# Relative position tiles: key units of the next tile alternate with query units of this one, and the square between them lies transposed in every other tile

## The reference

```python
dist_idx = pos_l - pos_r + M - 1
pos_emb = dist_emb[dist_idx]                            # [512, 512, 16]
rel_q = jnp.einsum('bhld,lrd->bhlr', q, pos_emb)
rel_k = jnp.einsum('bhrd,lrd->bhlr', k, pos_emb)
scores = (scores + rel_q + rel_k) / jnp.sqrt(D)
```

## Time and profile before

| | |
|---|---|
| median of 3 runs | 2111.92 us (2110.01 to 2112.20) |
| the profiled execution | 2123.17 us |
| its span in the trace | 2121.5 us |
| TensorE matmuls busy | 1641.8 us, 77% of the span |
| VectorE busy | 1129.5 us, 53% |
| ScalarE busy | 1032.1 us, 49% |
| DMA, mean over the span | 247 GB/s |
| TensorE's mean granted clock | 0.89 of full |

### The profile page before, as it was taken

The page is one execution under the profiler, slowest core; times in us unless marked ns, Lnnn a source line. Parts: engine busy times, 40 slices in busy tenths (PEclk is TensorE's granted clock), DMA queues, the critical chain, the costliest instruction groups (busy, mean ns, idle before and its releaser), DMA issues. The chain is left out here.

```text
span 2121.5 us, 32639 instructions
## 1 busy us (share of the span) xinstructions
PE 1641.8 (77%) x11256; PEld 1204.0 (57%) x11256; DVE 1129.5 (53%) x3008; ACT 1032.1 (49%) x2029; POOL 537.5 (25%) x628
## 2 busy tenths in 40 slices
PE   6758420089898899978899899858989989889881
PEld 3325320078787788767778788734555555555550
DVE  6666434213344444313444344447888887888860
ACT  3424304044343343443334344358887887887860
POOL 2343342200100000001010000053043644634534
PEclk9878655589999999979999999969999999999995
DMA  6574465688789678788887777589889989999831
GB/s 202 176 239 145 144 192 139 194 208 276 274 276 300 241 259 300 231 262 300 307 301 259 244 256 258 220 286 325 259 253 322 295 270 311 294 281 325 292 111 40
DMA packets 227380, 523.34 MB, mean 247 GB/s; under 512 B 37328, under 2 KB 83920, under 8 KB 221712
## 3 DMA queue, kind: packets, MB, share of 16 engines
q1 hardware_dynamic: 201856, 414.22, 60.3%
q0 software_dynamic: 24208, 98.65, 14.3%
q10 hardware_dynamic: 1152, 8.39, 1.0%
HBM read 371.27 MB, written 203.42 MB: 271 GB/s over the span
## 5 line engine op out<-in xcount | busy, mean ns | idle before, releaser
L986 DVE TENSOR_TENSOR rel_out<-rl,rel_tile 128x1024 f32<-128x1024 f32 x256 | 305.9, 1221 | 225.9 <-PE rl L1038 177.9
L1254 ACT ACTIVATE scores<-scores,row_least 128x512 f32<-128x512 f32 x512 | 365.6, 717 | 27.9 <-DVE row_least L1288 27.7
L1288 DVE CUSTOM_DVE_ANT_1 scores<-sc,rq 128x512 f32<-128x512 f32 x512 | 336.3, 687 | 33.6 <-issue 27.9
L1390 PE MATMUL pt<-ident,scores 128*128 128x128 f32 x2048 | 322.7, 281 | 34.0 <-ACT probsT L1259 17.5
L963 ACT COPY rel_tile<-rl 128x1024 f32<-128x1024 f32 x256 | 249.7, 1017 | 180.6 <-PE rl L1038 169.8
L1059 PE MATMUL up<-rowsT,w_b 128*128 128x256 f32 x1280 | 322.1, 396 | 3.3 <-DMA w_b<-in_w 3.3
L1072 PE MATMUL dn<-w_b,hid 128*128 128x256 f32 x1280 | 322.3, 396 | 0.0
L971 ACT ACTIVATE hid<-up,w_b 128x256 f32<-128x256 f32 x320 | 134.3, 471 | 375.5 <-PE up L1059 374.8
L1390 PEld LDWEIGHTS pt<-ident,scores 128*128 128x128 f32 x2048 | 250.4, 145 | 109.0 <-DVE probsT L1294 53.7
L1059 PEld LDWEIGHTS up<-rowsT,w_b 128*128 128x128 f32 x1280 | 237.9, 196 | 31.0 <-issue 3.6
L1072 PEld LDWEIGHTS dn<-w_b,hid 128*128 128x128 f32 x1280 | 239.4, 197 | 27.6
(11 more groups left out here) (186 smaller groups left out, 1654.4 us busy)
## 6 DMA issues: line engine op xcount, KB each, us to landing
scratch_rel<-rel_out SPq DMA_DIRECT2D x256, 512.0 KB, 4.5
rq<-scratch_rel SPq DMA_DIRECT2D x256, 512.0 KB, 6.5
krows_sb<-scratch_stack SPq DMA_DIRECT2D x768, 64.0 KB, 2.4
w_b<-in_w POOLq DMA_DIRECT2D x40, 1152.0 KB
w_b<-in_w POOLq DMA_DIRECT2D x40, 1028.0 KB
scratch_parts<-part SPq DMA_DIRECT2D x96, 128.0 KB
by_head<-scratch_parts SPq DMA_DIRECT2D x16, 768.0 KB, 5.8
scratch_stack<-by_row SPq DMA_DIRECT2D x4, 3072.0 KB, 25.4
```

The costliest lines, as they stand in the source:

```text
L986: nc.vector.tensor_tensor(out[n % SRING][:], rl[r][:].rearrange("p a (b s) -> p (a b) s", s=TILE), both[:, u * UN:(u + 1) * UN], ALU.add). ...
L1254: nc.scalar.activation(sm[j][:, i], sm[j][:, i], ACT.Exp, bias=least[:, j, i:i + 1], scale=-1.0, accum_out=es[:, g // 2 % 2, i, 2 * j + g ...
L1288: nc.vector.tensor_tensor_reduce(sm[j][:, i].rearrange("p (c s) -> p c s", c=LT), sc[i % 2][:].rearrange("p (c s) -> p c s", c=LT), rq[j][ ...
L1390: last = nc.tensor.transpose(pt[r % 2][:, i * P:(i + 1) * P], sm[n % HG][:, i, r * P:(r + 1) * P], ident[:])
```

## The change

The first key phase (16 units) stays as it was. After it, query unit u of a tile and key unit u of the next tile alternate; the last tile's query units come alone. Key unit u of tile t+1 is written over the part of the square that query unit u of tile t has just read. Since that part is 8 rows and a key unit delivers 8 columns, the square of every odd tile lies transposed: `square(tile)` gives the view. In an odd tile ScalarE therefore writes words 512 bytes apart, and VectorE reads its second operand in words 512 bytes apart.

```diff
+        def step(n):
+            m = n - UNITS
+            if m < 0:
+                return 0, 0, n, n % 2
+            tile, k = m // (2 * UNITS), m % (2 * UNITS)
+            if tile + 1 < TILES:
+                return (1, tile, k // 2, n % 2) if k % 2 == 0 else (0, tile + 1, k // 2, n % 2)
+            return 1, tile, k, n % 2
+        STEP_OF = {step(n)[:3]: n for n in range(TILES * 2 * UNITS)}
+        def square(tile):
+            return both[:] if tile % 2 == 0 else both[:].rearrange("p s l -> p l s")
...
             for n in range(x * total // spots, (x + 1) * total // spots):
-                tile, u = n // (2 * UNITS), n % (2 * UNITS)
-                yield u // UNITS, tile, u % UNITS, n % 2
+                yield step(n)
...
             for x in range(KRING):
                 load_k(x)
+            for p in range(PIECES):
+                load_q(0, p)
+            for p in range(PIECES - 1):
+                load_k(p + KRING)
             for tile in range(TILES):
-                for p in range(PIECES):
-                    if tile == 0:
-                        load_q(0, p)
-                    x = tile * PIECES + p + KRING
-                    if x < TILES * PIECES:
-                        load_k(x)
                 for u in range(UNITS):
                     ...
+                    x = ((tile + 1) * UNITS + u) // PER_PIECE - 1 + KRING
+                    if u % PER_PIECE == 0 and x < TILES * PIECES:
+                        load_k(x)
                     if tile % LT == LT - 1 and tile + 1 < TILES and u % PER_PIECE == PER_PIECE - 1:
                         load_q(tile // LT + 1, u // PER_PIECE)
...
                         act.wait_ge(s_kp, tile * UNITS + u + 1)
-                        after(act, s_qa, tile * UNITS)
-                        nc.scalar.copy(both[:, :, u * UN:(u + 1) * UN],
+                        if tile:
+                            act.wait_ge(s_qa, (tile - 1) * UNITS + u + 1)
+                        nc.scalar.copy(square(tile)[:, :, u * UN:(u + 1) * UN],
...
-                                                both[:, u * UN:(u + 1) * UN], ALU.add).then_inc(s_qa, 1)
+                                                square(tile)[:, u * UN:(u + 1) * UN], ALU.add).then_inc(s_qa, 1)
...
+                    if STEP_OF[side, tile, u] >= 2:
+                        was, its_tile, its_u, _ = step(STEP_OF[side, tile, u] - 2)
+                        pe.wait_ge((s_kc, s_qa)[was], its_tile * UNITS + its_u + 1)
```

More of the change, by code:

```diff
@@ L1017, in relative @@
                             pe.wait_ge(s_kl[x % KRING], (x // KRING + 1) * 16 * len(PAIRS))
[L1018 to L1021, removed]
                     else:
```

## The result

| | before | changed |
|---|---|---|
| median | 2112.06 us (2110.01 to 2112.53, 4 runs) | 2080.35 us (2078.49 to 2083.24, 4 runs) |
| ratio, 95% interval | | 0.9846 (0.9819 to 0.9873) |
| profiled execution | 2123.17 us | 2081.64 us |
| mean granted clock | 0.89 | 0.90 |

The changed kernel was run again later, beside others: 2080.1 us, ratio 0.9848 (0.9831 to 0.9865). Over all batches the kernel before spread from 2108 to 2130 us, the changed one from 2077 to 2083; kernels of different batches are therefore compared here by their ratio to the kernel before or by their traces.

What follows compares the result with a forecast made beforehand. TensorE, with late key rows and additions, bounds the experts stage: 132 us lost, less 40 for remaining lateness and 68 for strides, gives 24 us less: 2099 profiled, 2088 median. Range 2025 to 2135 us.

Steps and rivals of the forecast that it cites:

- TensorE sets the stage: Experts stage, 949 us: TensorE sets its length; forty clean blocks would take 817 us, so 132 us are lost.
- Late key rows and the clock behind them: Experts stage: TensorE waits 66.0 us for krows_sb; 43 us come from the lower clock after long waits.
- Start: Stage start: all 48 query-row transfers issue before key piece 3; wait of 11 us, 15 charged with the low clock.
- Rounds with query rows: Rounds 3, 7 and 11: SyncE needs 7.6 us per two pairs lasting 6.4; about 5 us a round, 15 charged.
- Weight bursts: Experts stage: weight bursts and the clock they cost, 10 us charged, bounds 0 and 25.
- Strided copies and additions: Odd tiles' transposed square: copies of 1.9 us and additions of 2.05 us, 68 us charged in all.
- the turns of tiles: Each turn of a tile: first addition and last copy wait for each other, about 8 us charged.
- The chain: Query product's end to free accumulator: 3.55 us with slow copy, 3.5 with slow addition, against 2.68 once in five spots.
- The sum: Whole kernel: 132 us given back less 40 and 68 charged, so 24 us less; median 2088 us.
- Rival 1: Square's copies and additions: strided access costs little on one engine or both; 2020, 2049 or 2059 us; chance 0.32.
- rival 2: ScalarE's strided write: copy of 2.4 us or more, deciding from about 2.3; gain gone, 2122 or 2154 us; chance 0.16.
- rival 3: SyncE's loads stay late: krows_sb waits keep some 25 us more with their clock; 2112 us; chance 0.12.

Runs made afterwards that it cites:

- the best version: Changed kernel with the square in 8 x 8 blocks, first query rows interleaved with key pieces, six key-row buffers instead of three: 2004.27 us, ratio 0.9494.
- the flat square: Changed kernel with the square kept as 16 slabs of adjacent words, transposition left out, so sums join wrong words: 2041.56 us, ratio 0.9636.
- ring of six: Six key-row buffers instead of three: in the kernel before 2067.47 us, ratio 0.9745; in the changed kernel 2061.41 us, ratio 0.9764.
- the blocked square: Changed kernel with the square kept in 8 x 8 blocks, only the order of blocks transposed in odd tiles: 2038.12 us, ratio 0.9663.

## Why the prediction was right, point by point

**TensorE sets the stage, 817 us if nothing is late.** Right: the best version comes within 14 us of it, and the flat square repeats the 102.1 us.

**Late key rows and the clock behind them.** Right in kind and size. The early loads took away all long waits but the first. The ring of six in the kernel before shows it from the other side, and shows what I had not priced: with the key rows on time, the bursts of stores become the next limit.

**Start, 15 us charged.** Direction right, size short. SyncE's issues there:

```profile
428.37 24.01 SPq L911 DMA_DIRECT2D qrows_sb<-scratch_stack  x48
452.42 22.69 SPq L906 DMA_DIRECT2D krows_sb<-scratch_stack  x35
```

The wait was foreseen as 11 us and was 17.0: the 48 query transfers took 24.0 us of issue from 428.37 on, and the key pieces' issues began at 452.42 (446.0 in my sum; the stage also began 4 us later). From there TensorE went on after 9.4 us, where my sum had 5.0 for issues and landing. I had taken the run's median landing of 2.4 us; between 425 and 462 us a key-row transfer took 6.0 us to land in the median, a query-row transfer 12.9. The rows had the warning: before, this piece took 13.7 us from 433.52 to 447.21. The first block took 41.25 us, 20.8 over a clean one.

**Rounds with query rows, 15 us.** The waits there sum to 9.1 us (0.52, 1.69 and 0.90 from 697 us on, 3.45 at 899.79, 2.55 at 1149.15); two of 1.79 and 1.36 stand elsewhere. SyncE's issues in the first of these rounds (start us, us, how many):

```profile
691.61 3.20 SPq L906 DMA_DIRECT2D krows_sb<-scratch_stack  x6
...
695.77 3.06 SPq L911 DMA_DIRECT2D qrows_sb<-scratch_stack  x6
698.88 0.42 SPq L924 DMA_DIRECT2D scratch_rel<-rel_out  x1
699.35 3.09 SPq L906 DMA_DIRECT2D krows_sb<-scratch_stack  x6
```

From one key piece to the next it is 7.74 us, as my 7.6 had it, with queries at 3.1 and keys at 3.1 rather than 3.88 and 2.8. The ring of six removes these waits. **Weight bursts, 10 us:** at most the 3 us elsewhere. Together the late rows after the second block lengthened their blocks by 13 to 14 us, where I had charged 25.

**Strided copies and additions, 68 us.** Prices right: 1.93 against my 1.9, 1.92 against 2.05. VectorE's addition paid 0.70 us for the hops, ScalarE's copy 0.92, as ScalarE's own bf16 row had said. The bf16 copy on VectorE at 1.14 ns an element was the misleading row; it differs in having one source and 2-byte words, and no run separates the two. The Trainium skill ("Vector Engine (DVE) Microarchitecture Reference", section 5.2) has 1.73 ns a column for a source with 4 KiB hops, from which I had estimated 1.9 us for the addition and, with the same increment, 1.7 for the copy. The trace's 1.92 agrees for VectorE; ScalarE's 1.93 is above the estimate.

What was mis-sized is what the slow instructions cost: 1.17 us x 36 blocks = 42 us in the rounds instead of 60, and 7.4 in the last tile (its two blocks 24.94 + 24.28 against 21.65 + 20.13 in the flat square) for my 8. An even round lost 3.8 us (I had 4.4), an odd one 2.1 (I had 3.4), and both figures already contain the turns of tiles, for which I charged 8 more. The chain itself was right: from the end of a query product (528.14) to the key unit that waits for the copy (531.63) it is 3.49 us against my 3.55, and the room is the 2.68 I had. The place is then 0.8 us late, and the further 0.2 I put in for the activations shows nowhere, since no wait for a copy is over 0.7 us. In odd rounds one of the four places is nearly free.

**The sum.** 24 us forecast, 32 measured. Charges of 108 against some 88: 23 start with the second block, 13 to 14 other late rows, 42 and 7 strides; the rest is that the first and last blocks are not mean ones. That the number came so near is partly luck. I had worked from the profiled execution, and there the stage got 44 us shorter and not 24. It stood 11 us above its median, so the medians show only 32 of it; and the start, charged too low, offset part of the strides, charged too high. The stage's end, 1334.98, is just inside the 1330 to 1365 I had set.

**Rival 1** fell with the durations; **rival 2** with a copy of 1.93 us, below its deciding point of 2.3; **rival 3** fell, though its place, SyncE in three rounds, was a true cost of about 9 us. The figure of 2.5 ns a column that the same page of the Trainium skill has for a destination with steps of 24 words did not show here: the copy, with steps of 128 words, took 1.88 ns an element with its overhead.

## What to carry to other kernels

Where an in-order queue holds stores that wait for results and loads for later work, put each load as far ahead as its buffer allows: a ring of six alone gave the kernel before 0.0255, more than the whole of this change. The alternation is worth about as much again (0.0251, with the same ring and start), because it also spreads the stores, but only once its strides cost nothing. A fine interleave makes short chains of waits through several engines: add up the chain for the closest pair in the order, not the busy time per pair, before lengthening an instruction in it. If a transposed layout seems to need single-word strides, transpose blocks instead and leave their inside alone.

## What the runs showed of the hardware

ScalarE writing float32 words 512 bytes apart takes 1.93 us for 1024 elements, against 1.01 in runs of 8 words with the same step from run to run. By the kernel's views all these copies read the accumulator in PSUM in words 512 bytes apart, those of 1.01 us too; it is the writing of single words that costs. VectorE reading one operand in such single words takes 1.92 against 1.22. In the blocked square it reads runs of 8 words with steps of 256 bytes or 4 KB between them, and no addition took longer than 1226 ns; I had allowed up to 1.25 us.

The many short waits left the granted clock at its upper level, the long ones did not. Windows of the changed kernel (us, busy PE, PEld, DVE, ACT, POOL, PEclk, DMA share, GB/s): a stretch whose waits, for the copy or key rows, are 1.8 us at most; the slice with most of the 17.0 us wait; and the one just after the wait of 3.45 us at 899.79:

```profile
480.00:880.00 400.00, 381.23 (x3122) 329.22 (x3121) 209.65 (x174) 230.65 (x263) 34.62 (x74) 1.00 0.83 277
440.00:460.00 20.00, 4.85 (x36) 3.99 (x35) 1.00 (x2) 3.97 (x7) 0.77 (x2) 0.71 1.05 260
900.00:920.00 20.00, 19.57 (x143) 16.84 (x142) 10.79 (x8) 6.64 (x9) 1.52 (x3) 0.86 0.99 350
```

In the first stretch TensorE stood 18.8 of 400 us, at a granted clock of 1.00. In the kernel before 89 us of waits, many of them long, came with a loss of 132.
